# Two value banks and two score banks in place of one and three, scores two blocks ahead, in an attention kernel with its loop written out

## What is computed

```python
xs = jnp.reshape(x, (B, T, C))                       # x here is the normalised input, T = 1024, C = 512
q = jnp.einsum('btc,hcd->bhtd', xs, Wq)              # 8 heads of 64
k = jnp.einsum('btc,hcd->bhtd', xs, Wk)
v = jnp.einsum('btc,hcd->bhtd', xs, Wv)
scores = jnp.einsum('bhtd,bhsd->bhts', q, k) * scale
att = jax.nn.softmax(scores, axis=-1)
out = jnp.einsum('bhts,bhsd->bhtd', att, v)
out = jnp.transpose(out, (0, 2, 1, 3)).reshape(B, T, -1)
out = out @ Wproj + bproj
# result: x + out, x as it came in
```

## Time and profile before

| what | value |
|---|---|
| median of 3 runs | 4596.09 us (4592.58 to 4597.46) |
| the profiled execution | 4596.62 us |
| its span | 4594.8 us |
| mean granted TensorE clock | 0.996 of full speed |
| busy: PE, PEld, DVE, ACT, POOL | 97%, 79%, 58%, 64%, 62% |
| HBM | 30 GB/s over the span |

### The profile page before, as it was taken

One profiled execution on the slowest core, in us unless ns is written; L12 is line 12 of the kernel. 1 busy time (PEld: TensorE's weight loads), 2 busy tenths in 40 slices (PEclk: granted clock), 3 DMA queues, 4 the chain that ended last, 5 costly groups with the idle time before them and its releaser, 6 DMA issues.

```text
span 4594.8 us, 74513 instructions
## 1 busy us (share of the span) xinstructions
PE 4467.0 (97%) x20864; PEld 3620.3 (79%) x20864; DVE 2666.6 (58%) x5030; ACT 2957.0 (64%) x5637; POOL 2826.7 (62%) x2221
## 2 busy tenths in 40 slices
PE   7999999999999999999999999999999999999998
PEld 5878778787787877878778788777787778877786
DVE  5664746656466564655646556465564656647553
ACT  4765757657576675766757667575675756657575
POOL 2656756666566565665656656566565665566567
PEclk9999999999999999999999999999999999999999
DMA  2111111111111111121111111211112121121101
GB/s 73 34 42 60 35 58 37 44 56 34 57 38 52 48 38 53 37 58 42 37 58 34 59 42 35 67 29 61 39 33 67 30 61 37 32 67 38 57 23 56
DMA packets 157005, 213.29 MB, mean 46 GB/s; under 512 B 56544, under 2 KB 57568, under 8 KB 156512
## 3 DMA queue, kind: packets, MB, share of 16 engines
q1 hardware_dynamic: 156512, 207.47, 15.9%
HBM read 105.12 MB, written 34.08 MB: 30 GB/s over the span
## 4 chain that ended last, share of the span: by engine, by line
PE 89%; DVE 5%; issue 3%; ACT 2%; DMA 1%; POOL 1%; SPq 0%; DVEq 0%; ACTq 0%; POOLq 0%
PE bank L653 15%; PE bank L706 10%; PE bank L699 9%; PE bank L700 9%; PE bank L852 9%; PE bank L854 9%; PE bank L853 9%; PE bank L665 8%; PE bank L684 8%; DVE smax L1042 1%; PE bank L671 1%; DMA den<-acc 1%; ACT prob_h L870 1%; DVE xs L1009 1%; DVE k_hl L1023 1%
## 5 line engine op out<-in xcount | busy, mean ns | idle before, releaser
L1204 POOL TENSOR_TENSOR prob_l<-prob,prob_h 128x512 fp32r<-128x512 f32 x1664 | 2140.0, 1297 | 1659.2 <-ACT prob_h L870 1640.0
L1042 DVE TENSOR_REDUCE smax<-bank 128x1 f32<-128x512 f32 x2048 | 1346.9, 683 | 776.5 <-PE bank L706 763.2
L870 ACT ACTIVATE prob<-bank 128x512 f32<-128x512 f32 x2048 | 1234.8, 603 | 787.2 <-PE bank L700 656.2
L870 ACT ACTIVATE prob_h<-bank 128x512 fp32r<-128x512 f32 x2048 | 1228.9, 600 | 452.5 <-PE bank L854 422.3
L852 PE MATMUL bank<-prob_h,vh 128*128 128x512 f32 x2048 | 823.3, 402 | 25.3 <-ACT acc L955 22.8
L699 PE MATMUL bank<-q_hh,k_hl 128*128 128x512 f32 x2048 | 826.0, 403 | 1.3 <-issue 0.8
L700 PE MATMUL bank<-q_lm,k_h 65*128 65x512 f32 x2048 | 809.9, 395 | 0.0
L854 PE MATMUL bank<-prob_l,vh 128*128 128x512 f32 x2048 | 807.9, 394 | 0.0
L853 PE MATMUL bank<-prob_h,vl 128*128 128x512 f32 x2048 | 807.9, 394 | 0.0
L706 PE MATMUL bank<-k_hl,q_hh 128*128 128x512 f32 x2048 | 717.8, 403 | 26.3 <-DVE smax L1042 15.8
L980 DVE TENSOR_TENSOR prob_l<-prob,prob_h 128x512 fp32r<-128x512 f32 x384 | 331.5, 863 | 379.0 <-ACT prob_h L870 376.8
(11 more groups left out here) (68 smaller groups left out, 5094.8 us busy)
## 6 DMA issues: line engine op xcount, KB each, us to landing
xs<-in_x SPq DMA_DIRECT2D x256, 256.0 KB, 2.8
q_hh<-q_hh SPq DMA_DIRECT2D x256, 128.0 KB, 2.2
k_hl<-k_h SPq DMA_DIRECT2D x256, 128.0 KB, 2.4
inv_b<-inv_dram SPq DMA_DIRECT2D x256, 128.0 KB, 2.8
out_x<-xs SPq DMA_DIRECT2D x128, 256.0 KB, 2.0
q_lm<-q_lm SPq DMA_DIRECT2D x256, 2.0 KB
den<-acc SPq DMA_DIRECT2D x256, 2.0 KB, 1.8
inv_dram<-inv SPq DMA_DIRECT2D x256, 2.0 KB, 1.3
```

Source lines behind the costliest of these rows:

```text
L870: return nc.scalar.activation(out, ps[ST + bank][:, :], ACT.Exp, scale=SCALE)
L1042: nc.vector.tensor_reduce(smax[:, 2 * t + half:2 * t + half + 1], ps[SM + turn][:, :], AX.X, ALU.max).then_inc(rows_used, 1)
L1204: nc.gpsimd.tensor_tensor(prob_l[:, r3, :], prob[:, ring2, :], prob_h[:, r3, :].bitcast(F32), ALU.subtract).then_inc(prob_l_pool, 1)
```

## The change

- Score banks are 0 and 1, chosen by the block's parity; value banks are 2 and 3, one for each half of the queries; turn banks are 4 and 5. `AHEAD` is 2.
- ACT: `prob` of block i+2 once the low part of block i is made; `prob_h` of block i+2 once the value matmuls of block i-1 are done. `copy_out` stays between the two exponentials of slots 7 and 15. `early` is gone.
- PE: the first value matmul of a half waits for the copy of the same half of the head before.
- `WORK`, `LATE`, `OUT_SLOTS`, `POOL_BLOCKS` are as before, so with `AHEAD` 2 a slot's exponentials and low part are those of one block earlier than before. In the last head DVE has 7 low parts and POOL 9 (`END_POOL`).
- The loop is written out: 120 heads in a row on each engine, waits on constants.
- Prologue: all eight token tiles are loaded at once (the last four into the buffers of `prob` and `acc`), their statistics are taken together, and the eight transposes follow each other. The casts of the weights are cut in parts, and POOL makes their low parts. The value matmuls stand between the row scores; `turn_rows` comes after the tenth, and the first two scores after the fourteenth.
- End: POOL adds four biases and splits the fourth tile ahead of the last `normalise`.

```diff
-ST, SM, PVB, WB = 0, 3, 5, 6
+ST, SM, PVB, WB = 0, 4, 2, 6
-AHEAD = 3
+AHEAD = 2
+END_POOL = (1, 3, 5, 6, 8, 9, 11, 13, 15)
...
         def run(eng, step):
-            step(Step(eng, 0, "first", 0, plan, B, None))
-            with eng.Fori(0, B - 1) as it:
-                bases = {}
+            step(Step(eng, 0, "first", 0, plan))
+            for it in range(B - 1):
                 for k in range(1, 9):
-                    step(Step(eng, it, "body", k, plan, B, bases))
+                    step(Step(eng, it, "body", k, plan))
...
         def ring3(s, i):
-            return (BLOCKS * s.h + i) % (BLOCKS * NH) % 3
-
-        def early(s, i):
-            return int(s.h == 7 and i + AHEAD - BLOCKS in (0, 1))
+            return s.heads(BLOCKS, 0, i) % 3
...
# tensor, step
-                            pe.wait_ge(prob_h_ready, s.heads(BLOCKS, 0, i + 1 + early(s, i)))
+                            pe.wait_ge(prob_h_ready, s.heads(BLOCKS, 0, i + 1))
...
-                        scores((s.k + ahead) % 2, j, ring3(s, i + AHEAD), wait)
+                        scores((s.k + ahead) % 2, j, j % 2, wait)
...
-                        pe.wait_ge(acc_ready, s.heads(2, 0, tc))
+                        if not (first or s.h == 0 and s.section == "body" and s.k == 0):
+                            pe.wait_ge(acc_ready, s.heads(2, -1, tc + 1))
...
-                    bank = PVB
+                    bank = PVB + tc
...
# scalar, step
                         act.wait_ge(scores_ready, s.heads(BLOCKS, ahead, j + 1))
-                        lo_wait(act, s, i + 1)
-                        exp_to(prob[:, j % 2, :], r3)
+                        lo_wait(act, s, i)
+                        exp_to(prob[:, j % 2, :], j % 2)
                     if i % TT == TT - 1:
                         copy_out(s, i // TT)
                     if not (end and ahead):
-                        act.wait_ge(pv_done, s.heads(BLOCKS, 0, i + 1 + early(s, i)))
-                        exp_to(prob_h[:, r3, :], r3).then_inc(prob_h_ready, 1)
+                        if not (first and i == 0):
+                            act.wait_ge(pv_done, s.heads(BLOCKS, 0, i))
+                        exp_to(prob_h[:, r3, :], j % 2).then_inc(prob_h_ready, 1)
...
# tensor, prologue
+            for t in range(TT):
+                start_entry("xt", t, wait=lambda: pe.wait_ge(xn_ready, t + 1))
...
             for j in range(BLOCKS):
-                if j >= 2:
+                if j == 11:
+                    pe.wait_ge(mt_used, 1)
+                elif j == 10:
+                    pe.wait_ge(rows_used, 10)
+                elif j >= 2:
                     pe.wait_ge(rows_used, j - 1)
-                row_scores(0, j, j % 2)
-            pe.wait_ge(nmax_ready, 1)
-            pe.wait_ge(rows_used, BLOCKS)
-            turn_rows(0, 0)
-            start_entry("v", 2)
+                row_scores(0, j, (j + (j > 9)) % 2)
+                until = 9 * (j + 1) // 2
+                while v_units < until:
+                    a, lo = divmod(v_units, UNITS["v"])
+                    hi = min(lo + until - v_units, UNITS["v"])
+                    start_entry("v", a, lo=lo, hi=hi)
+                    v_units += hi - lo
...
             start_entry("v", 3)
...
# vector, step
-                    if s.h == 7 and i == 14 and not end:
-                        lo_part(0, ring3(s, 13 + AHEAD), lambda: dve.wait_ge(prob_h_ready, s.heads(BLOCKS, 1, 1)))
-                    if j not in POOL_BLOCKS and not (end and ahead) and not (s.h == 7 and i == 13):
+                    if j not in pool_blocks_of(s, ahead) and not (end and ahead):
...
# gpsimd, prologue and end
+            for c in range(CH):
+                pool.wait_ge(w_hi, c + 1)
+                nc.gpsimd.tensor_tensor(wqk_l[:, c, :, :], raw_qk[:, c, :, :], wqk_h[:, c, :, :].bitcast(F32),
+                                        ALU.subtract).then_inc(w_lo, 1)
...
             for t in range(SPLIT):
                 split_out(s, t)
+            for t in range(2):
+                add_bias(s, t)
+            split_out(s, SPLIT)
+            for t in range(2, RES):
+                add_bias(s, t)
             normalise(s, -1, 1)
-            for t in range(TT):
+            for t in range(SPLIT + 1, TT):
+                split_out(s, t)
                 add_bias(s, t)
-                if t + SPLIT < TT:
-                    split_out(s, t + SPLIT)
```

More of the change, by code:

```diff
@@ L411, in attention_block @@
         x_in = [sem(f"x_in{t}") for t in range(4)]
+        first_in = [sem(f"first_in{t}") for t in range(4)]
         res_in = [sem(f"res_in{n}") for n in range(RES)]
@@ L455, in attention_block, with pool_blocks_of @@
         per_dve = BLOCKS - per_pool
+        def pool_blocks_of(s, ahead):
+            return END_POOL if s.section == "last" and s.k + ahead == NH - 1 else POOL_BLOCKS
         def lo_wait(eng, s, i):
             ahead, i = divmod(i, BLOCKS)
-            if i in POOL_BLOCKS:
-                eng.wait_ge(prob_l_pool, s.heads(per_pool, ahead, POOL_BLOCKS.index(i) + 1))
+            pool_blocks = pool_blocks_of(s, ahead)
+            if i in pool_blocks:
+                eng.wait_ge(prob_l_pool, s.heads(per_pool, ahead, pool_blocks.index(i) + 1))
             else:
-                n = sum(j not in POOL_BLOCKS for j in range(i + 1))
+                n = sum(j not in pool_blocks for j in range(i + 1))
                 eng.wait_ge(prob_l_ready, s.heads(per_dve, ahead, n))
@@ L625, in _ @@
             run(sp, step)
-            s = Step(sp, B - 1, "last", 8, plan, B, None)
+            s = Step(sp, B - 1, "last", 8, plan)
             den_to_square(s, -1, 1)
@@ L640, in _, with entry @@
         def _(pe):
-            def entry(kind, a, lo, hi, bank, before, head, wait):
+            def entry(kind, a, lo, hi, bank, before, head, wait, tile=None):
                 w = ps[WB + bank]
@@ L858, in _ @@
             run(pe, step)
-            s = Step(pe, B - 1, "last", 8, plan, B, None)
+            s = Step(pe, B - 1, "last", 8, plan)
             for t in range(TT):
@@ L968, in _ @@
             run(act, step)
-            s = Step(act, B - 1, "last", 8, plan, B, None)
+            s = Step(act, B - 1, "last", 8, plan)
             for t in range(TT):
@@ new lines, in _ @@
+            take_mean(start_bank("mean", 1), 2, lambda n: n + 11, 4)
+            take_var(start_bank("var", 1), 2, 4)
+            for t in range(4):
+                norm(t, first_x(t), 1)
+            for t in range(4):
+                start_take("xt", t)
+                norm(4 + t, first_x(4 + t), 2)
+            for t in range(4, 8):
+                start_take("xt", t)
+            start_take("qk", 0)
+            start_take("qk", 1)
+            start_take("qn", 0)
+            for j in range(BLOCKS):
+                take_max(j, j + 1, (j + (j > 9)) % 2)
+                if j == 1:
+                    start_take("qn", 1)
+                if j == 6:
+                    start_take("v", 0)
+                if j == 7:
+                    combine(0, 8)
+                if j == 9:
+                    take_rows(0, 0, 1)
+                if j == 11:
+                    start_take("v", 1)
@@ L1172, in _ @@
             run(dve, step)
-            s = Step(dve, B - 1, "last", 8, plan, B, None)
+            s = Step(dve, B - 1, "last", 8, plan)
             reciprocal(s, -1, 1)
@@ L1218, in normalise @@
                 if s.slots is None:
-                    pool.wait_ge(o_split, s.batches(TT, SPLIT))
+                    pool.wait_ge(o_split, s.batches(TT, SPLIT + 1))
+                    pool.wait_ge(res_bias, s.batches(TT, RES))
                 end = s.h == 7 and not s.has_next
-                blocks = 0 if s.slots is None else min(s.out_slots[tc] + 1 + AHEAD, BLOCKS if end else 99)
-                pool.wait_ge(prob_l_pool, s.heads(per_pool, 0, sum(j % BLOCKS in POOL_BLOCKS for j in range(blocks))))
+                if s.slots is None:
+                    pool.wait_ge(prob_l_pool, s.heads(per_pool, -1, len(END_POOL)))
+                else:
+                    blocks = min(s.out_slots[tc] + 1 + AHEAD, BLOCKS if end else 99)
+                    done = sum(j % BLOCKS in pool_blocks_of(s, j // BLOCKS) for j in range(blocks))
+                    pool.wait_ge(prob_l_pool, s.heads(per_pool, 0, done))
                 pool.wait_ge(inv_in, s.heads(32, ahead, 16 * (tc + 1)))
@@ L1244, in step @@
                     ahead, j = divmod(i + AHEAD, BLOCKS)
-                    if j in POOL_BLOCKS and not (end and ahead):
+                    if j in pool_blocks_of(s, ahead) and not (end and ahead):
                         lo_part(j % 2, ring3(s, i + AHEAD), s.heads(BLOCKS, ahead, j + 1))
```

250 lines of the change are left out of this document (129 added, 121 removed).

## The result

| | time (median) | against before |
|---|---|---|
| before | 4594.34 us (4591.61 to 4597.46) | |
| the changed kernel | 4620.88 us (4619.25 to 4622.51) | 1.0058 [1.0040, 1.0075] |
| its profiled execution | 4621.34 us, span 4619.5, granted clock 1.0 | |

What follows compares the result with a forecast made beforehand. The prediction took PE, busy 97% of the span, and its waits to bound the kernel; 4596.6 - 28 (loop) + 93 (banks, scores two ahead) - 19 (prologue) - 8 (end) gave 4635 us, range 4570 to 4680.

Runs made afterwards that it cites:

- e6_b8: The changed kernel with block 8's low part made by DVE and not by POOL; 4728.29 us, 1.0294 [1.0278, 1.0310].

## What to carry to other kernels

A buffer that lets work run ahead is worth what it hides at the tightest places of the period, and these can be found beforehand: the time that the full engine leaves at each place, against the chain measured on the others. When a bank or a distance changes, look again at what was placed where only because of it: the copy stood first for the sake of the single value bank, and moving it gave 27 us. Price a stall from start to start over all its occurrences, look at the granted clock behind it, and run the parts of a change apart: this one hid -47 and -22 behind +94.

## What was not expected of the hardware

- A back-jump of PE costs 2.17 us from start to start (1.7 to 2.5). Behind 4 of 14 the clock stood at its lower level for 3.4 us, which made them 1.5 to 2.1 us dearer. The jumps of the other engines at the same place cost nothing on the path.
- DVE instructions with two inputs in SBUF stretch from 0.68 to as much as 1.8 us beside a POOL instruction, and a float32 TENSOR_SCALAR from SBUF to SBUF from 0.53 to 1.39 in the mean. Those with an input in PSUM do not, and neither does the one that takes statistics from a single SBUF input (BATCH_NORM_STATS2, never over 0.70, 122 of them beside POOL).
- In e6_b8 PE's clock fell behind the wait of 2.38 us. The stretches (columns as above) around the wait and behind it:

```profile
2050.00:2054.00 4.00, 2.31 (x13) 1.65 (x11) 1.43 (x3) 1.76 (x6) 1.18 (x1) 1.00 0.28 66
2054.00:2057.00 3.00, 2.31 (x12) 2.31 (x13) 2.62 (x7) 0.00 (x0) 0.00 (x0) 0.68 0.00 0
2057.00:2060.00 3.00, 3.00 (x17) 2.71 (x17) 0.00 (x0) 1.12 (x3) 0.00 (x0) 0.75 0.00 0
```

Behind the wait the 256-wide matmuls follow each other every 0.21 us, where it was 0.12 ahead of it: for 3.4 us the clock stood at the lower of the two levels, 1.2 GHz, and then again at 2.4. So the 3.79 us at that place are more than the wait: in the three batches of the 14 without a fall there (1, 5 and 10) the place loses 2.66 us, in the eleven with one 3.3 to 4.6.
